# A mixing and low-rank kernel on one core: weights laid out in longer rows, first loads reordered, identity matmuls at the start, and other PSUM banks for the last two batches

## The reference

```python
x = x + einsum('bct,bcd->bdt', x, weights[condition])      # one of 16 matrices 128x128 per batch
Bx  = einsum('bni,bri->bnr', x, B[adapter_ids])            # rank 16, contraction over the 2048 times
x = x + einsum('bnr,bor->bno', Bx, A[adapter_ids]) * 1.0   # one of 64 adapters per batch
```

## Time and profile before

| what | value |
|---|---|
| median of three runs | 401.35 us (400.98 to 402.23) |
| the profiled execution's own time | 401.69 us |
| its span, first to last instruction | 399.8 us |
| PE busy | 379.0 us, 95% |
| DVE / ACT / POOL busy | 68% / 55% / 7% |
| DMA | 152.4 MB, 381 GB/s over the span |

### The profile page before, as it was taken

How to read it: one execution, slowest core, us unless ns; L and a number is a source line. 1 busy time by engine, 2 the same in 40 slices (tenths; PEclk the granted TensorE clock), 3 DMA queues, 4 the chain that set the end, 5 groups by cost and what they waited for, 6 DMA issues and landing times.

```text
span 399.8 us, 16408 instructions
## 1 busy us (share of the span) xinstructions
PE 379.0 (95%) x6144; PEld 349.7 (87%) x6144; DVE 271.3 (68%) x576; ACT 221.7 (55%) x513; POOL 29.8 (7%) x71
## 2 busy tenths in 40 slices
PE   1999999999999999999999999999999999999962
PEld 1899999999999999999999999999999999999951
DVE  0067677668667767766866776776686677678684
ACT  1465565566556556556555655555555565565540
POOL 1110000000000000000000000000000000000000
PEclk9999999999999999999999999999999999999995
DMA  7999999999999999999999999999999999999546
GB/s 224 331 421 380 403 391 409 390 418 395 406 402 393 404 399 415 396 402 407 398 398 403 415 381 407 402 405 403 404 406 394 409 403 397 404 403 371 233 185 236
DMA packets 29777, 152.37 MB, mean 381 GB/s; under 512 B 3268, under 2 KB 3524, under 8 KB 13764
## 3 DMA queue, kind: packets, MB, share of 16 engines
q1 hardware_dynamic: 29764, 152.19, 96.6%
HBM read 85.07 MB, written 67.11 MB: 381 GB/s over the span
## 4 chain that ended last, share of the span: by engine, by line
PE 91%; DMA 3%; DVE 2%; SPq 2%; issue 1%; DVEq 0%; ACT 0%
PE f_bank L314 58%; PE low_bank L344 17%; PE z_bank L328 15%; DMA x_in<-in_x 3%; DVE x_out L247 2%; SPq L127 0%; DVE z_pair L273 0%; SPq L130 0%; SPq L135 0%; SPq L115 0%; SPq L131 0%; SPq L121 0%; DVE z_all L278 0%; DVE at L265 0%; DVEq L49 0%
## 5 line engine op out<-in xcount | busy, mean ns | idle before, releaser
L314 PE MATMUL f_bank<-m_sel,x_in 128*128 128x128 f32 x2048 | 247.7, 280 | 9.4 <-POOL m_sel L183 8.4
L314 PEld LDWEIGHTS f_bank<-m_sel,x_in 128*128 128x128 f32 x2048 | 235.6, 193 | 17.1 <-issue 9.3
L205 ACT COPY ft<-f_bank 128x512 f32<-128x512 f32 x256 | 149.8, 586 | 81.8 <-PE f_bank L314 80.7
L247 DVE TENSOR_TENSOR x_out<-low_bank,ft 128x512 f32<-128x512 f32 x256 | 158.9, 682 | 4.3 <-PE low_bank L344 2.4
L273 DVE TENSOR_TENSOR z_pair<-z_bank,z_two 16x128 f32<-16x128 f32 x128 | 36.8, 287 | 105.2 <-ACT z_two L213 103.1
L344 PE MATMUL low_bank<-z_all,at 16*128 16x128 f32 x2048 | 76.0, 285 | 5.3 <-DVE x_out L247 5.3
L344 PEld LDWEIGHTS low_bank<-z_all,at 16*128 16x128 f32 x2048 | 63.8, 188 | 18.8 <-issue 18.8
L328 PE MATMUL z_bank<-ft,ab_in 128*16 128x128 f32 x2048 | 68.3, 274 | 0.0
L221 ACT COPY z_all<-z_all 16x128 f32<-16x128 f32 x128 | 37.8, 296 | 51.1 <-DVE z_all L278 49.5
L328 PEld LDWEIGHTS z_bank<-ft,ab_in 128*16 128x16 f32 x2048 | 50.3, 96 | 7.8 <-issue 0.2
L177 POOL TENSOR_TENSOR m_sel<-w_all,ident 128x128 f32<-128x128 f32 x62 | 28.1, 454 | 317.4 <-PE f_bank L314 285.1
(11 more groups left out here) (1 smaller groups left out, 0.0 us busy)
## 6 DMA issues: line engine op xcount, KB each, us to landing
x_in<-in_x SPq DMA_DIRECT2D x63, 1024.0 KB, 9.2
out<-x_out SPq DMA_DIRECT2D x62, 1024.0 KB, 7.2
ab_in<-in_lora SPq DMA_DIRECT2D x64, 256.0 KB, 8.0
out<-x_out SPq DMA_DIRECT2D x8, 256.0 KB, 2.9
x_in<-in_x SPq DMA_DIRECT2D x4, 256.0 KB, 4.1
w_first<-in_L_cond_weights SPq DMA_DIRECT2D x2, 64.0 KB, 5.0
ids<-in_itok_B SPq DMA_DIRECT2D x2, 0.2 KB
w_all<-in_L_cond_weights SPq DMA_DIRECT2D x1, 0.5 KB, 9.0
```

The source lines that it names most:

```text
L205: nc.scalar.copy(ft[k][u][:], f_bank[BANK_OF[u]][:]).then_inc(copied, 1)
L247: nc.vector.tensor_tensor(x_out[k][:, UNIT * u:UNIT * (u + 1)], low_bank[u][:], ft[k][u][:], ALU.add).then_inc(added, 1)
L314: last = nc.tensor.matmul(f_bank[BANK_OF[u]][:, P * c:P * (c + 1)], x_in[k][:, UNIT * u + P * c:UNIT * u + P * (c + 1)], m_sel[k][:], star ...
```

## The change

All 16 matrices are laid out by the host as 128 x 16 x 128, so that a partition's 8 KB lie in one row; the two lists of integers come as one input. SP's first loads stand in another order: lists, first unit of x 0, `w_first` 0, rest of x 0 in one DMA, x 1, `w_first` 1, `ab_in` 0, `w_all`, x 2, `ab_in` 1, x 3, `ab_in` 2, `ab_in` 3. PE multiplies the identity by itself ten times before its first mix. `at` has four buffers, and `turn_a` runs two batches ahead instead of one. In the last two batches the low rank goes to other banks: batch 62 to `f_bank` 0 to 2 and `low_bank` 3, batch 63 to `low_bank` 0 to 2 and `z_bank`; the additions of batch 61 are split in two halves (`LATE`: units 3 and 0, then 1 and 2), with `sum_tiles` of batch 63 between them. The arithmetic is the same. The diff's core:

```diff
+LATE = (3, 0, 1, 2)
+WARM_UP = 10
-        at = [sbuf(f"at{i}", [P, JS, BLOCK]) for i in range(2)]
+        at = [sbuf(f"at{k}", [P, JS, BLOCK]) for k in range(BODY)]
+        late_banks = [f_bank + low_bank[UNITS - 1:], low_bank[:UNITS - 1] + [z_bank]]
+        def banks_of(b):
+            return late_banks[b - (BATCHES - 2)] if isinstance(b, int) and b >= BATCHES - 2 else low_bank
 @block.sync
-            sp.dma_start(ids[0:1, 0, :], cond_ids).then_inc(ids_in, 16)
-            sp.dma_start(ids[0:1, 1, :], adapter_ids).then_inc(ids_in, 16)
-            for u in range(UNITS):
-                cols = slice(UNIT * u, UNIT * (u + 1))
-                sp.dma_start(x_in[0][:, cols], x[0, :, cols]).then_inc(first_loaded[u], 16)
-            sp.wait_ge(ids_in, 32)
-            for k in range(2):
+            def load_first(i):
+                cols = slice(0, UNIT) if i == 0 else slice(UNIT, TIME)
+                sp.dma_start(x_in[0][:, cols], x[0, :, cols]).then_inc(first_loaded[i], 16)
+            def load_w_first(k):
                 cond = sp.value_load(ids[0:1, 0, k:k + 1], min_val=0, max_val=CONDITIONS - 1)
-                sp.dma_start(w_first[k][:], weights[cond]).then_inc(w_first_in[k], 16)
-                load_ab(k, adapter_of(k))
-                if k == 0:
-                    load_x(1, 1)
-            sp.dma_start(w_all[:], weights.rearrange("m c d -> c m d")).then_inc(w_in, 16)
+                sp.dma_start(w_first[k][:], weights[:, cond, :]).then_inc(w_first_in[k], 16)
+            sp.dma_start(ids[:].rearrange("p n b -> p (n b)"), both_ids).then_inc(ids_in, 16)
+            load_first(0)
+            sp.wait_ge(ids_in, 16)
+            load_w_first(0)
+            load_first(1)
+            load_x(1, 1)
+            load_w_first(1)
+            load_ab(0, adapter_of(0))
+            sp.dma_start(w_all[:], weights).then_inc(w_in, 16)
             for k in range(2, BODY):
                 load_x(k, k)
-                load_ab(k, adapter_of(k))
+                load_ab(k - 1, adapter_of(k - 1))
+            load_ab(BODY - 1, adapter_of(BODY - 1))
 @block.vector
             turn_a(0, 0, 1)
+            turn_a(1, 1, 1)
             def turn(q, last):
-                for k in range(BODY):
+                for k in range(BODY - 2 if last else BODY):
                     sum_tiles(k, b)
                     if begun(b - 1):
-                        add_batch((k - 1) % BODY, b - 1, q - (k == 0))
-                    if exists(k + 1, last):
-                        turn_a((k + 1) % BODY, b + 1, q + (k + 1) // BODY + 1)
-                if last:
-                    add_batch(BODY - 1, BATCHES - 1, TURNS - 1)
+                        add_units((k - 1) % BODY, range(UNITS), b - 1, q - (k == 0))
+                    turn_a((k + 2) % BODY, b + 2, q + (k + 2) // BODY + 1)
+            sum_tiles(BODY - 2, BATCHES - 2)
+            add_units(BODY - 3, LATE[0:2], BATCHES - 3, TURNS - 1)
+            sum_tiles(BODY - 1, BATCHES - 1)
+            add_units(BODY - 3, LATE[2:], BATCHES - 3, TURNS - 1)
+            add_units(BODY - 2, range(UNITS), BATCHES - 2, TURNS - 1)
+            add_units(BODY - 1, range(UNITS), BATCHES - 1, TURNS - 1)
 @block.tensor
-                if live(b):
+                if isinstance(b, int) and b == BATCHES - 2:
+                    pe.wait_ge(added, UNITS * (b - 1) + 1)
+                elif isinstance(b, int) and b == BATCHES - 1:
+                    pe.wait_ge(added, UNITS * (b - 1))
+                    pe.wait_ge(z_paired, 2 * BATCHES)
+                elif live(b):
                     pe.wait_ge(added, UNITS * b)
+            pe.wait_ge(ident_made, 1)
+            for _ in range(WARM_UP):
+                nc.tensor.matmul(f_bank[2][:, 0:P], ident[:], ident[:], start=True, stop=True)
 def kernel(**inputs):
+    given = {"x": ..., "weights": np.asarray(inputs["L0_cond_weights"]).transpose(1, 0, 2)}
+    given["ids"] = np.stack([np.asarray(inputs["itok_B_0_15"]), np.asarray(inputs["itok_B_4_50"])]).reshape(1, -1)
```

More of the change, by code:

```diff
@@ L45, in begun, with cond_lora_residual @@
     return not (isinstance(b, int) and b < 0)
-def cond_lora_residual(nc, x, cond_ids, adapter_ids, weights, lora, out):
+def cond_lora_residual(nc, x, both_ids, weights, lora, out):
     with ExitStack() as ctx:
@@ L83, in cond_lora_residual @@
         w_first_in = [sem(f"w_first_in{k}") for k in range(2)]
-        first_loaded = [sem(f"first_loaded{u}") for u in range(UNITS)]
+        first_loaded = [sem(f"first_loaded{i}") for i in range(2)]
         x_loaded = [sem(f"x_loaded{k}") for k in range(BODY)]
@@ L177, in pick_m @@
                 nc.gpsimd.tensor_tensor(m_sel[k][:], w_all[:, cond, :], ident[:], ALU.add).then_inc(m_picked, 1)
-            pool.wait_ge(ids_in, 32)
+            pool.wait_ge(ids_in, 16)
             pool.wait_ge(ident_made, 1)
@@ L244, in _, with add_unit, add_units @@
         def _(dve):
-            def add_unit(k, u):
-                nc.vector.tensor_tensor(x_out[k][:, UNIT * u:UNIT * (u + 1)], low_bank[u][:], ft[k][u][:],
+            def add_unit(k, u, b):
+                nc.vector.tensor_tensor(x_out[k][:, UNIT * u:UNIT * (u + 1)], banks_of(b)[u][:], ft[k][u][:],
                                         ALU.add).then_inc(added, 1)
-            def add_batch(k, b, turns):
+            def add_units(k, units, b, turns):
                 if live(turns):
@@ L254, in add_batch @@
                 dve.wait_ge(low_done, b + 1)
-                for u in range(UNITS):
-                    add_unit(k, u)
+                for u in units:
+                    add_unit(k, u, b)
             def turn_a(k, b, turns):
                 dve.wait_ge(ab_loaded[k], 16 * turns)
-                if live(b - 1):
-                    dve.wait_ge(low_done, b - 1)
+                if live(b - BODY + 1):
+                    dve.wait_ge(low_done, b - BODY + 1)
                 flat = ab_in[k][:, 0:JS * RANK + RANK]
                 blocks = bass.AP(flat.tensor, flat.offset, [flat.ap[0], [RANK, JS], [1, BLOCK]])
-                nc.vector.transpose(at[k % 2][:], blocks).then_inc(a_turned, 1)
+                nc.vector.transpose(at[k][:], blocks).then_inc(a_turned, 1)
             def sum_tiles(k, b):
@@ L304, in mix_unit @@
                 if isinstance(b, int) and b == 0:
-                    pe.wait_ge(first_loaded[u], 16)
+                    pe.wait_ge(first_loaded[min(u, 1)], 16)
                 elif u == 0:
@@ L343, in add_low_rank @@
                         js = slice(c * (P // BLOCK), (c + 1) * (P // BLOCK))
-                        last = nc.tensor.matmul(low_bank[u][:, P * c:P * (c + 1)],
-                                                at[k % 2][rows, js, :].rearrange("r j i -> r (j i)"),
+                        last = nc.tensor.matmul(banks_of(b)[u][:, P * c:P * (c + 1)],
+                                                at[k][rows, js, :].rearrange("r j i -> r (j i)"),
                                                 z_all[k % 2][rows, :], start=(c == 0), stop=(c == IN_UNIT - 1),
@@ L368, in _ @@
             turn(TURNS - 1, True)
-_INS = ['x', 'itok_B_0_15', 'itok_B_4_50', 'L0_cond_weights']
+_INS = ['x', 'ids', 'weights', 'lora']
 def laid_out_b(b):
@@ L391 @@
     nc = bacc.Bacc("TRN2", target_bir_lowering=False, num_devices=1)
-    given = {name: np.asarray(inputs[name]) for name in _INS}
+    given = {"x": np.asarray(inputs["x"]), "weights": np.asarray(inputs["L0_cond_weights"]).transpose(1, 0, 2)}
+    given["ids"] = np.stack([np.asarray(inputs["itok_B_0_15"]), np.asarray(inputs["itok_B_4_50"])]).reshape(1, -1)
     given["lora"] = np.concatenate([laid_out_a(np.asarray(inputs["L1_cond_A"])),
@@ L395 @@
     arrays, args = {}, []
-    for name, a in given.items():
-        if name.startswith("itok"):
-            a = a.reshape(1, -1)
-        a = np.ascontiguousarray(a)
+    for name in _INS:
+        a = np.ascontiguousarray(given[name])
         arrays[f"in_{name}"] = a
```

## The result

The changed kernel takes 398.6 us (four runs, 398.51 to 398.63), the one before 401.59 beside it: ratio 0.9925, 95% interval 0.9908 to 0.9942. The profiled execution took 398.63 us with a span of 396.8, against 401.69 and 399.8. So 398.5 was as good as met. The two parts of the sum were not: the start gave 2.7 us instead of 1.7, the end 0.4 instead of 1.2.

The account below looks back on a forecast made before the run. PE's own work was taken to bound the loop, leaving gains only ahead of mix 3 and behind the last `sum_z`. 401.69 - 1.7 - 1.2 = 398.8 profiled, 0.34 above the median: 398.5 us, range 396.0 to 400.9.

Parts of the forecast that it names:

- the start: Loads and first mixes up to mix 3: mix 3 starts at 24.3 instead of 26.0, -1.7 us (bounds -2.4, 0).
- the end: Behind the last `sum_z`: last addition 3.0 us earlier, but stores queue, so -1.2 us; -0.5 at 373 GB/s, -3.0 without queue.
- Index, first mix, rest of x 0: Start: `w_first` 0 issued at 3.2, PE starts about 6.5, 1.9 us earlier; other three x units land at 8.1.
- Identity matmuls: Before mix 0: ten cost 2.2 us, 1.5 to 3.7, while PE waits; whether they raise the clock hardly matters.
- the wait for `ab_in` 1: Mix 2: `ab_in` 1 lands at 18.2, `turn_a` 1 holds DVE, then ACT; PE's unit 3 loses 0.7 us.
- Mix 1: Start: waits for `w_first` 1, landing at 12.1 by 2.23 MB at 219 GB/s; starts at 12.7, ends at 16.5.
- x 2: Start: 8 KB rows of `w_all` save 0.95 us; x 2 lands at 17.6, mix 2 starts at 17.7, 2.4 us earlier.
- Rival A: Start: 512 byte rows cost nothing, or x 2 late otherwise; x 2 at 18.5, start -0.8, 399.4 us; chance 0.15.
- Rival D: Start: SP's full queue delays `ab_in` 1 to 21.4, holding DVE; mix 3 +1.6, 402.9 us without end gain; chance 0.07.
- `turn_a` two ahead in the loop: Loop: `turn_a` runs one batch earlier at no cost; `ab_in` lands 8.0 us after issue, turned after 11.7, cover 3.7 us.

Follow-up runs that it names:

- the halves: The changed kernel with batches 62 and 63 stored in two halves of 512 KB (rows of 4 KB) each instead of four units (rows of 2 KB): 397.19 us.

## Why the prediction was right, and where it was not

The total was right by luck, because two errors cancelled: -1.7 and -1.2 were forecast, -2.66 and -0.4 came (401.69 - 3.06 = 398.63), the one beyond its bound of -2.4, the other short of the -0.5 at 373 GB/s.

- **Index, first mix, rest of x 0:** `w_first` 0 issued at 3.10 (3.2), PE at 6.34 (6.5), units 1 to 3 at 8.15 (8.1). Right.
- **Identity matmuls: the step failed.** They were taken as ten instructions of 0.216 us, over at 3.7. They are 20 (the 32 of a mix are likewise 16 calls in the code), take 4.46 us and end at 6.02, 0.3 us ahead of mix 0, which then runs at the full rate (24 in 2.94). The row of the end that spoke against the clock's rise had a burst of 1.17 us behind idleness; it was not the same case. The conclusion, that it hardly matters here, held (0.1 us), and by a reason given: the wait for `ab_in` 1 absorbs it.
- **Mix 1: this step failed too.** It was to wait for `w_first` 1, in at 12.1, and to start at 12.7. It came at 11.86, and what it waited for was ACT's copy of mix 0 (0.77 us); `w_first` 1 was there at 10.9. The kernel before shows the same wait:

```profile
15.13 3.81 PE L314 MATMUL f_bank<-m_sel,x_in 128*128 128x128 f32 x32 [0.77 <-ACT ft L205]
```

The rate behind the 12.1 was too low as well. The 219 GB/s count only the 2.49 MB that stood in the queue up to `w_first` 1; the slices of the earlier trace rows add up to 3.4 MB by 13.6, so loads issued behind it were moving at the same time.
- **x 2: mis-sized.** For the rows 0.95 us was taken, from 294 against 401 GB/s; the run with short rows puts mix 2 1.7 and `ab_in` 1 2.8 us later. x 2 was there by 16.6 instead of 17.6, level with the end of `sum_z` 0. In the kernel before the two had been as close: PE waited only 0.18 us for x 2, so that its own late start set the end nearly as much, as the run with the rows alone shows.
- **Rival A:** it would have the rows change nothing. The run with short rows took 401.05, at 348 GB/s against 419 in the same stretch at full share. The Trainium skill ("DMA: Bandwidth & Descriptors", "Specifications") states that 512 bytes are enough for line rate; this run does not agree with it.
- **`ab_in` 1:** forecast 0.7 us lost in mix 2, seen 0.60 ahead of its last unit, and 0.9 in the run without it. Right. Rival D was not met, because SP's issue of x 2 took 0.45 us; with the short rows it took 4.22, and the loss grew as D says.
- **`turn_a` two ahead in the loop:** no cost seen; PE 60.00 of 60.00 us. It was not run apart.
- **The end: additions right, stores mis-sized.** The last addition is 3.06 earlier (3.0), low rank 62 right behind the first addition of 61. But the stores did not go at the 401 of the loop: they went at 315 and 366 GB/s at first and at 327 and 295 with the engines full. The nearest row, 373 with rows of 8 KB among them, had been named as a bound and was still a little too high. That holding back half of batch 61 starts the queue 1.4 us later against `sum_z` than the old order (issued at 385.81, and at 384.33 in the run with the old end) stood in the sum as 388.35 against 387.05, but its price, a longer idle stretch of the DMA engines, was not drawn out. The expectation of the halves counts 270 GB/s as full share; that window has a share of 0.71.

What the kernel could still give was in the prediction as costs: the wait for `ab_in` 1 and the store queue. Taking the first away and shortening the second gives 394.91.

## What to carry to other kernels

Where two things end at nearly the same time, an edit to one alone shows nothing, and so does its removal: rows without order 401.56, order without rows 401.05, both 398.6 (order here means all the rest of the change); the identity matmuls 0.1 or 1.7, the edit of the end 0 or about 3. Before an edit is dropped as worthless, take away what stands level with it and measure again. At the end of a kernel count the bytes still to be stored, from the first moment at which any of them is ready: finishing the arithmetic sooner gains only what the store queue lets through. Half a tile stored early (1.35 us) or fewer stores with rows twice as long (1.45 us) were worth more here.

## What the runs showed of the hardware

- Stores in rows of 2 KB went at 327 and 295 GB/s with the DMA engines full (390 to 394 in the changed kernel), half as many stores in rows of 4 KB at 404 and 406 in the same stretch. In the loop, mixed loads and stores in rows of 8 and 2 KB went at 401.
- A load of 1 MB in 2048 pieces held SP for 4.22 us in the next DMA's issue (0.45 us with 128 rows), so it delayed loads that stood far behind it. In the kernel before, the same issue took 4.60 us.
- Loads do not land one after another: by 13.6 us of the kernel before 3.4 MB had moved, of which only 2.49 MB stood in the queue up to `w_first` 1.
- One float32 matmul of the code is two on PE, in the identity matmuls (20 for 10) as in the mixes.
- The clock column read 1.00 while the first matmuls of the kernel before took 0.216 us each; at the start only the matmuls' own spacing tells the rate.
